# The last expert's rows completed from PSUM behind the combine of all tokens, in a fused decoder layer on one core

## The reference, cut to what matters

```python
S, E, C = 2048, 8, int(1.25 * 2048 / 8)          # C = 320 slots for each expert
logits = xf @ gate_w + gate_b
probs = jax.nn.softmax(logits, axis=1)
topk_p, topk_i = jax.lax.top_k(probs, 2)         # two experts for each token
topk_pn = topk_p / jnp.sum(topk_p, axis=1, keepdims=True)
...                                              # idx[e, slot] = token, first come first served
h = jax.nn.relu(jnp.einsum('ecd,edh->ech', xin, w1) + b1[:, None, :])   # 256 -> 1024
out = jnp.einsum('ech,ehd->ecd', h, w2) + b2[:, None, :]                # 1024 -> 256
out = out * jnp.where(valid, tok_w, 0.0)[:, :, None]
final = jnp.zeros((S + 1, d), xf.dtype).at[idx.reshape(-1)].add(out.reshape(-1, d))[:S]
...
x = _layernorm(x + final)                        # the layer's output
```

## Time and profile before

| | |
|---|---|
| median of 3 runs | 482.84 us (482.6 to 483.24) |
| the profiled execution's own time | 481.71 us |
| its span in the trace | 479.9 us |
| busy in the span | PE 83%, DVE 77%, ACT 51%, POOL 30% |
| mean granted TensorE clock | 0.905 of full speed |

### The profile page before, as it was taken

The page is one execution under the profiler, slowest core; times in us unless marked ns, Lnnn a source line. Parts: engine busy times, 40 slices in busy tenths (PEclk is TensorE's granted clock), DMA queues, the critical chain, the costliest instruction groups (busy, mean ns, idle before and its releaser), DMA issues.

```text
span 479.9 us, 13542 instructions
## 1 busy us (share of the span) xinstructions
PE 400.0 (83%) x4673; PEld 307.8 (64%) x4673; DVE 367.2 (77%) x1555; ACT 243.0 (51%) x787; POOL 146.2 (30%) x240
## 2 busy tenths in 40 slices
PE   8999998899999999999997782269999999997000
PEld 4666776787888878888885672137677777675000
DVE  5678988678888888888888257859788898793284
ACT  1452676234433443433434244448889988861053
POOL 0033346513122030311303010142353355322384
PEclk9999999799999999999999685559999999999555
DMA  8673101901102011020110000072566446001582
GB/s 282 215 243 120 56 2 66 338 18 35 55 0 77 11 33 55 0 87 0 34 46 23 1 3 23 23 223 54 185 215 212 135 139 221 29 25 33 170 279 100
DMA packets 38238, 46.36 MB, mean 97 GB/s; under 512 B 4155, under 2 KB 32702, under 8 KB 38202
## 3 DMA queue, kind: packets, MB, share of 16 engines
q1 hardware_dynamic: 34474, 35.80, 23.0%
q0 software_dynamic: 3200, 9.40, 6.0%
q10 hardware_dynamic: 528, 0.69, 0.5%
HBM read 34.91 MB, written 11.01 MB: 96 GB/s over the span
## 4 chain that ended last, share of the span: by engine, by line
PE 56%; DVE 16%; ACT 8%; issue 7%; DMA 7%; POOL 4%; SPq 1%; ACTq 0%; DVEq 0%; POOLq 0%
PE bank L870 55%; DMA xin_t<-in_xT 2%; DMA wbuf<-in_w 2%; ACT arena L773 2%; ACT arena L782 1%; ACT kp L782 1%; DVE h L1328 1%; PE bank L1242 1%; DVE ub L1317 1%; DMA wbuf<-ybuf 1%; DVE mb L1319 1%; ACT arena L812 1%; DVE vp L1712 1%; DVE arena L1732 1%; DMA bz<-in_b_rows 1%
## 5 line engine op out<-in xcount | busy, mean ns | idle before, releaser
L623 ACT ACTIVATE rzb<-bank 128x32 f32<-128x32 f32 x128 | 25.5, 200 | 97.7 <-PE bank L870 97.5
L870 PE MATMUL bank<-h,whp 128*128 128x32 f16 x1143 | 59.1, 184 | 0.0
L870 PE MATMUL bank<-arena 128*128 128x320 f16 x384 | 57.4, 308 | 1.4 <-DVE arena L1759 1.4
L870 PE MATMUL bank<-arena,kp 128*128 128x320 f16 x384 | 54.5, 299 | 0.0
L1317 DVE TENSOR_TENSOR_SCAN ub<-rzb,bank 128x32 f32<-128x32 f32 x128 | 28.0, 219 | 29.6 <-ACT rzb L623 27.5
L626 ACT ACTIVATE nb<-ub 128x16 f32<-128x16 f32 x128 | 27.9, 218 | 44.0 <-DVE ub L1317 44.0
L870 PEld LDWEIGHTS bank<-arena 128*128 128x128 f16 x384 | 38.3, 102 | 17.1 <-DVE arena L1759 1.6
L870 PEld LDWEIGHTS bank<-arena,kp 128*128 128x128 f16 x384 | 37.3, 98 | 14.1
L870 PEld LDWEIGHTS bank<-h,whp 128*128 128x128 f16 x1143 | 40.7, 97 | 8.0
L577 POOL DMA_INDIRECT ybuf<-arena,six x24 | 24.2, 1008 | 58.0 <-DVE arena L1774 53.1
L870 PEld LDWEIGHTS bank<-hsb,at_w 66*64 66x64 f32 x256 | 25.4, 136 | 24.1 <-DVE hsb L1323 12.2
(11 more groups left out here) (214 smaller groups left out, 939.3 us busy)
## 6 DMA issues: line engine op xcount, KB each, us to landing
wbuf<-in_w SPq DMA_DIRECT2D x16, 1024.0 KB, 5.8
ybuf<-zero POOLq DMA_DIRECT2D x8, 512.0 KB, 7.2
wbuf<-ybuf SPq DMA_DIRECT2D x16, 256.0 KB, 5.8
xin_t<-in_xT SPq DMA_DIRECT2D x16, 128.0 KB, 2.3
arena<-in_ctxT SPq DMA_DIRECT2D x4, 512.0 KB, 7.4
xfin_t<-in_xT SPq DMA_DIRECT2D x16, 128.0 KB, 2.2
xres<-in_xtok SPq DMA_DIRECT2D x16, 128.0 KB, 2.1
x_d<-x SPq DMA_DIRECT2D x8, 256.0 KB, 2.3
```

The lines of the kernel that those rows point to most:

```text
L623: nc.scalar.activation(od(rzb[:]), RZ[j][:, s * 2 * B:(s + 1) * 2 * B], ACT.Sigmoid).then_inc(q["r_ready"], 1)
L870: return nc.tensor.matmul(out_, lhsT, rhs, start=start, stop=stop, skip_group_check=True)
```

## The change

All tokens are now combined without the last expert: its rows are not scattered to `ybuf`, where those rows stay zero, and SP's loads wait for the scatters of the first seven experts alone (and until the raw weights in the same buffer have been used). `results_T(6)` and `results(6)` stand earlier in expert 7. The tokens in the last expert's 320 slots are then made a second time and in full, slot by slot: their two weights come from a new small DRAM tensor `wt_d` (one DMA on SP writes it, `pairs` on POOL gathers it), and their other choice is gathered from `ybuf` (`others`, POOL). `fix_first` on DVE weights the other choice and adds x2, before chunk 1; `fix_second` adds the last expert's result straight from PSUM and takes the statistics, before chunk 3; `fix_rstd` on POOL stands behind `rstd_3(3)`; ACT applies the factors behind chunk 4; and `fixed` on POOL scatters the 320 rows over the output once all eight stores have landed. Five small DVE operations for the indices stand before the loop over experts 4 and 5. Some semaphores were merged to make room (`hscale` into `wsplit`, `ctx_load` and `yl0` to `yl3` into `quarter`), with the same waits.

```diff
+            sp.wait_ge(q["x2_st"], 16 * CHUNKS)
+            sp.wait_ge(q["ws_ready"], 4)
+            sp.dma_start(wt_d.rearrange("(k p) j -> p k j", p=P), wtp[:]).then_inc(q["x2_st"], 16)
...
+            sp.wait_ge(q["w_lo"], 4 * E)
             for j in range(2):
-                sp.wait_ge(q[f"yst{j}"], 16 * CT * (E // 2))
+                sp.wait_ge(q[f"yst{j}"], 16 * CT * (E // 2 - j))
...
+            sp.wait_ge(q["fix_st"], 16 * CT)
...
+            def pairs():
+                pool.wait_ge(q["x2_st"], 16 * (CHUNKS + 1))
+                for c, m, col in slots(E - 1):
+                    pool.indirect_dma_start(
+                        fwp[0:m, c, :], None, wt_d[:, :], bass.IndirectOffsetOnAxis(ap=gix[0:m, col], axis=0),
...
+            def others():
+                for j in range(2):
+                    pool.wait_ge(q[f"yst{j}"], 16 * CT * (E // 2 - j))
+                pool.wait_ge(q["xtr_ready"], E - 1)
+                pool.wait_ge(q["fix"], 4)
+                for c, m, col in slots(E - 1):
+                    pool.indirect_dma_start(
+                        xe[0][0:m, c, :], None, ybuf[:, :], bass.IndirectOffsetOnAxis(ap=oix[0:m, c:c + 1], axis=0),
...
+            def fix_rstd():
+                pool.wait_ge(q["fix"], FIX_VAR)
...                                               # four small operations, as in rstd_3
+            def fixed():
+                pool.wait_ge(q["fix_ready"], CT)
+                for r in range(3):
+                    pool.wait_ge(q[f"ost{r}"], 16 * len(range(r, CHUNKS, 3)))
+                for c, m, col in slots(E - 1):
+                    pool.indirect_dma_start(
+                        out[:, :], bass.IndirectOffsetOnAxis(ap=tix[0:m, c:c + 1], axis=0), yt[0][0:m, c, :], None,
...
+                if e == E - 2:
+                    pairs()
                 if e >= 1:
                     scatter(e - 1)
-            scatter(E - 1)
+            others()
...
+                if c == FIX_AT:                    # POOL, FIX_AT = 3
+                    fix_rstd()
+            fixed()
...
+                if last:                           # ACT, behind the last hidden piece, ahead of the wait for y_mm
+                    weighted(0)
+                    weighted(1)
                 act.wait_ge(q["y_mm"], e + 1)
...
+                if c == FIX_AT + 1:                # ACT, behind chunk 4
+                    act.wait_ge(q["fix_rstd"], 4)
+                    for k in range(CT):
+                        nc.scalar.activation(yt[0][0:m, k, :], yt[1][0:m, k, :], ACT.Identity,
+                                             bias=nm4[0:m, k:k + 1], scale=rs4[0:m, k:k + 1]).then_inc(q["fix_ready"], 1)
...
+                    if f == 2 and last_:           # PE, hidden pieces of expert 7
+                        pe.wait_ge(q["yT_ready"], 2 * e)
+                        pe.wait_ge(q["yt_ready"], 2 * e - 2)
+                        results_T(e - 1)
...
+            for j in range(2):
+                nc.vector.tensor_tensor(wtp[:, :, j], top[:, :, j], wsum[:], ALU.mult).then_inc(q["ws_ready"], 1)
...
+                    if f == 4 and last:            # DVE, hidden pieces of expert 7
+                        results(e - 1, 1 - j, 16 * CT * i)
...
-            results(E - 1, 1, 16 * CT * (E // 2 - 1))
...
+            def fix_first():
+                dve.wait_ge(q["pair_ready"], 16 * CT)
+                fix(nc.vector.tensor_tensor(fd[:], fwp[:, :, 1], fwp[:, :, 0], ALU.subtract))
+                fix(nc.vector.tensor_tensor(fd[:], fd[:], fj[:], ALU.mult))
+                nc.vector.tensor_tensor(f7[:], fwp[:, :, 0], fd[:], ALU.add)
+                fix(nc.vector.tensor_tensor(fo[:], fwp[:, :, 1], fd[:], ALU.subtract))
+                dve.wait_ge(q["other_ready"], 16 * CT)
+                for c, m in parts():
+                    last = nc.vector.scalar_tensor_tensor(xe[1][0:m, c, :], xe[0][0:m, c, :], fo[0:m, c:c + 1], xe[1][0:m, c, :],
...
+            def fix_second():
+                dve.wait_ge(q["ytr_ready"], E)
...                                               # 3 scalar_tensor_tensor from banks 0 and 1, 3 bn_stats, 3 bn_aggr
             for c in range(CHUNKS):
+                if c == 1:
+                    fix_first()
+                if c == FIX_AT:
+                    fix_second()
```

More of the change, by code:

```diff
@@ L813, in hidden, with weighted @@
                                      bias=b1s[j][:, f:f + 1]).then_inc(q["h32_ready"], 1)
+            def weighted(c):
+                act.wait_ge(*loaded(c))
+                nc.scalar.activation(yg[c][:, 0, :], yg[c][:, 0, :], ACT.Copy, scale=wt[:, 0, 2 * c:2 * c + 1]).then_inc(q["c_w"], 1)
             def expert(i, j):
@@ L1287, in expert @@
                                       f == n == 0, f == FK - 1 and n == 2)
-                    if f == 3 and not first:
-                        if not last_:
-                            pe.wait_ge(q["xlo_ready"], 2 * e + 4)
-                        else:
-                            pe.wait_ge(q["yt_ready"], 2 * e - 2)
+                    if f == 3 and not (first or last_):
+                        pe.wait_ge(q["xlo_ready"], 2 * e + 4)
                         results_T(e - 1)
@@ L1791, in expert @@
                         w_low(e + 1, 1 - j, p)
-                    if p == 3 and not (isinstance(e, int) and e == 0):
+                    if p == 3 and not last and not (isinstance(e, int) and e == 0):
                         pi = i if j else i - 1
@@ L1804, in _, with fix @@
             expert(1, 1)
+            at = [0]
+            def fix(ins):
+                at[0] += 1
+                ins.then_inc(q["fix"], 1)
+                dve.wait_ge(q["fix"], at[0])
+            own = slice((E - 1) * CT, E * CT)
+            fix(nc.vector.scalar_tensor_tensor(fd[:], gix[:, own], 2.0, v2[:, own], ALU.mult, ALU.subtract))
+            fix(nc.vector.tensor_scalar(oix[:], fd[:], float(S + 1), None, ALU.add))
+            fix(nc.vector.tensor_tensor(fj[:], v2[:, own], gix[:, own], ALU.subtract))
+            fix(nc.vector.tensor_tensor(tix[:], gix[:, own], v1[:, own], ALU.add))
+            fix(nc.vector.tensor_scalar(fj[:], fj[:], -1.0, 1.0 / S, ALU.add, ALU.mult))
             with dve.Fori(2, E // 2 - 1) as i:
```

85 lines of the change are left out of this document (61 added, 24 removed).

## The result

The changed kernel took 496.39 us (median of 4 runs, 494.71 to 497.75), the kernel before 483.04 us (4 runs, 482.6 to 484.01). The ratio is 1.0251, with a 95% interval of 1.0215 to 1.0287: slower by 13.4 us, where 3.3 us were forecast, and outside the range. The profiled execution took 496.15 us.

A forecast was written before the change was run, and what follows sets the result against it. PE bounds until expert 7's end, then a serial chain, then DVE, POOL and their loop with ACT nearly alike. Terms: -9.6 + 2.75 - 1.0 + 3.0 + 2.2 + 5.5 + 0.5 = +3.35 us, forecast 486.1 us; range 482.6 to 489.6.

The forecast's parts named there:

- term 6: Beside expert 0's gathers: wt_d's 2048 pieces of 8 bytes delay the rows PE waits for, +0.5 us.
- term 5: At the end: the last scatters wait for the last store, then are issued and land, +5.5 us, up to +8.0.
- term 1: Expert 7 into the tail: earlier transposes, copies and scatters let the first load start earlier, -9.6 us.
- term 2: Tail, ahead of chunk 1: fix_first without a wait for gathers, +2.75 us; chunks 1 and 2 give back 1.0 us.
- signs of being wrong: Chunks after fix_second under 2.45 us, DVE waiting long for the other choices, or yT so late that fix_second waits.
- Term 3: Tail, ahead of chunk 3: fix_second's work on DVE is hidden by nothing, +3.0 us.
- Term 4: Tail: fix_rstd on POOL ahead of first_choice(5), +1.4 us, and ACT's three operations ahead of chunk 5, +0.8 us.
- (a): Faster: the tail's inserted work is absorbed, POOL and ACT catching up during fix_second; 481.2 us, chance 0.18.
- (b): No change: POOL's and ACT's inserts alone are absorbed during fix_second, wt_d costs nothing; 483.5 us, chance 0.12.
- The rest costs nothing: Five small DVE operations ahead of expert 4 and pairs on POOL fall into idle time; without cover, 1 us each.
- (c): Slower still, by wt_d: expert 0 starts 3.4 us late; 489.1 us, chance 0.08.
- (d): Slower still, by landings: tail gathers at 9.6 (+1.9) and last scatters at 3.5 (+1.3); 489.4 us, chance 0.10.

The follow-up runs named there:

- e6: The changed kernel without wt_d and without the three small gathers (pairs) that read it: 496.56 us against 483.6.
- e10: The kernel of e1 with DVE's copies of expert 6's results back behind the last split of expert 7: 494.01 us against 484.06.
- e12: The changed kernel with only the early copies, scatters and loads, nothing of the second pass: 474.53 us against 484.06, ratio 0.9802.
- e7: The kernel of e1 with fix_first ahead of chunk 2 instead of chunk 1: 491.38 us against 483.6, ratio 1.0154.
- e9: The kernel of e1 without fix_rstd on POOL and without ACT's three operations: 491.87 us against 483.6.
- e3: The changed kernel without its last three scatters: 488.32 us against 484.01, ratio 1.0101.
- e5: The changed kernel with its last three scatters going to a spare tensor without waiting for the output's stores: 491.95 us against 483.6.
- e11: The kernel before with one indirect DMA of 64 rows to a spare tensor as POOL's last work: 485.32 us against 484.06.
- e1: The changed kernel with wt_d written behind the loads of the last experts' weights: 493.56 us against 484.01, ratio 1.0217.
- e2: The kernel before with only wtp's two small DVE operations and the DMA writing wt_d added: 487.69 us against 484.01, ratio 1.0074.
- e8: The changed kernel with wt_d's 16 KB written as 128 pieces of 128 bytes instead of 2048 of 8: 490.49 us against 484.06.
- e4: The kernel before with the change's startup edits only (hscale merged into wsplit, two memsets, wider epst): 484.29 us against 484.01, ratio 1.0020.

## Why the prediction was wrong

The direction was right and held the likeliest chance, and the list of what would be paid was right; the size was wrong by 10 us and lay outside the range. Without its first line the ledger exceeds the forecast by 8.3 us: 4.0 by term 6, 2.85 by term 5, 1.4 by term 1 and 1.35 by term 2, less 0.6 by terms 3 and 4 and 0.7 in the experts. The steps that failed are the price of wt_d and the end of the program. By the prediction's own steps:

- **Term 1, the early loads: -8.2, forecast -9.6.** Each step holds but one. "POOL's first scatter comes 0.77 us behind the copies, its third 2.57 us later" took the issue's length from a place where DVE was idle. At the early place, beside a DVE without gaps, the first issue took 2.40 us, and the 1.4 us went straight into the path (e6, e10, e12). The other issues of the trace of before, also those beside a busy DVE, gave no sign of it. yT was late as forecast, and fix_second didn't wait for it.
- **Term 2, fix_first: +4.7 - 1.6 = +3.1, forecast +2.75 - 1.0 = +1.75.** "I take the median: no wait" failed: the last gather landed 6.4 us after its issue, next to the worst row, 6.3, and DVE waited 1.84 us, the bound of 1.9. The whole insert took 4.29 us with the wait, 2.45 without it (forecast 2.3, where the parts named, 0.6 and 1.35, make 1.95). The rule of the Trainium skill, "DMA: Bandwidth & Descriptors", section "SWDGE vs HWDGE vs iDMA", that an engine serves its queues in turn doesn't keep the wait at 0 here. But the wait isn't the whole error: e7 took it away, and chunk 3 came 0.27 us earlier only. In e7 chunk 1 started 1.0 us later than before all the same, since its data came late, and the cause of that is open. Of the signs of being wrong that the prediction named, two were seen: the wait for the other choices, and chunks 3 and 4 behind fix_second, which took 2.14 and 2.11 us and not 2.45.
- **Term 3, fix_second: +2.7, forecast +3.0.** From 462.21 to 464.91. Right.
- **Term 4: +1.9, forecast +2.2** (e9). Right; it shows as DVE's wait of 1.98 us for POOL. Rivals (a) and (b), in which POOL and ACT catch up, are out: the inserts are paid in full. Terms 2 to 4 together are 7.7, forecast 6.95.
- **Term 5, the last scatters: +8.35, forecast +5.5.** The path that I summed is 0.98 + 2.67 + 2.1 = 5.75 us, so 0.2 off. What is missing is the step that had no row: I let the 1.6 us behind the last landing stay as they were. With indirect DMAs as POOL's last work they became 4.2, by a barrier of 3.9 us in place of 1.3 (e3, e5, e11).
- **Term 6, wt_d: +4.5, forecast +0.5.** This is the largest error. I had three numbers: 6.5 us by the price of a packet, 0.4 us if one small piece passes for each gathered row, and bounds of 0 and 3.4. I took 0.5, "nearer to the packets' row", which it was not: the packets' row said 6.5 us over the whole time of the gathers, and 0.5 was the guess that a gather meets few of the pieces. The bound was wrong too: 6.3 - 2.9 supposed that the slowest gather of before was as slow as a gather can be. The 6.3 us were a gather of expert 1, beside a load of weights, while expert 0's, for which PE waits, had 2.7 to 2.9. With wt_d expert 0's took 7.2 us, and PE's wait ended when wt_d landed (e1, e2, e8).
- **"The rest costs nothing"** holds: pairs and the five small operations show nowhere (e6 has the stages of e1).
- **The sum** was made against one execution with a high clock (0.905); the one after had 0.891. These 2.5 us are in the ledger's first line and go with a stretch at the lower clock that comes without the change too (e4). The runs' medians differ by 13.4 us and the ledger without that line by 11.7; the rest I put down to the clock in the same way, which is argued and not shown.

Of the rivals, (c) came true beyond its price: 4.5 us where it took 3.4. (d) had the wait for the gathers right (1.84 us where it took 1.9). Its price for the end, 6.8 us, is nearer to the 8.35 measured than mine, but by luck: it expected landings of 3.5 us, and the last scatters landed after 2.1 to 2.5. I had given each rival its chance as if only one could come, and the range ended at the dearer of them.

## What to carry to other kernels

Look at how a DMA is cut into pieces, and not at its bytes alone: 2048 pieces in 16 KB were a transfer of 8 us that slowed each gather beside it. A bound for such a collision is not the slowest landing seen so far; the price of its packets, 6.5 us, would have held. Work behind the last store is paid whole, with issue, landing and a longer program end. To be cheap, a second pass would have to end inside the stores that are there anyway, and not with an indirect DMA on POOL. And when a gain frees a fixed time, first try it alone (here 9.5 us) and then add up all that it needs: here 4.5 + 7.7 + 8.35 us.

## What the runs showed of the hardware

- An indirect DMA as POOL's last work made the end of the program longer, even where it landed before the last store: the last barrier took 2.4 us with one DMA of 64 rows (one execution) and 3.6 to 3.9 with three (320 rows, eight kernels), against 1.1 to 1.6 in five kernels without.
- Ten of POOL's issues of an indirect DMA took 2.1 to 2.4 us in place of about 1.0. All ended 0.86 to 0.89 us behind the end of a stretch in which DVE was never idle. But 249 other issues inside such stretches took 0.93 to 1.19 us, so DVE's work alone doesn't foretell it.
- A gather of 64 or 128 rows of 1 KB landed in 2.6 to 3.0 us in most executions with little beside it (up to 3.7 in two), 3.0 to 7.2 beside a load of 1 MB of weights, 4.7 to 7.0 under the tail's loads of 4 MB, and 6.9 to 8.1 beside 2048 pieces of 8 bytes. The same 16 KB in 128 pieces of 128 bytes left it at 2.6 to 2.9.
- The same program ran in 481.4 to 485.5 us. The runs with a mean granted clock of 0.900 or more had a median of 482.0 us, the others 484.4.
